# Normalising softmax probabilities on GpSimd: one two-operand multiply of 128x512, or four multiplies by a scalar of 128x128

## The reference, cut to what matters

```python
x = x + xattn(layernorm(x), ctx, ctx, q_norm_w, k_norm_w, w_out)
x = x + ffn(layernorm(x), ...)           # 512 -> 2048 -> 512, 4-bit weights, LoRA terms
# inside xattn: 16 query heads of 32 channels, 4 key/value heads
scores = where(causal, einsum('bgnqd,bgkd->bgnqk', q, k) * scale, -1e30)
attn   = softmax(scores, axis=-1)        # 16 heads x 128 queries x 128 keys a batch
out    = einsum('bgnqk,bgkd->bgnqd', attn, v)
```

## Time and profile before

| what | value |
|---|---|
| three runs | 483.17, 485.31, 486.15 us; median 485.31 us |
| the profiled execution's own time | 484.46 us |
| its span, first to last instruction | 482.7 us, so 1.8 us lie around it |
| busy: DVE, ACT | 352.0 us (73%), 300.3 us (62%) |
| mean granted TensorE clock | 0.979 |
| multiply by the inverse sums (L506), all 64 | 72.7 us of POOL |
| low part of the probabilities (L515), all 64 | 80.9 us of POOL |
| cast of the probabilities (L722), all 64 | 39.7 us of ACT |

### The profile page before, as it was taken

The page is one execution under the profiler, slowest core; times in us unless marked ns, Lnnn a source line. Parts: engine busy times, 40 slices in busy tenths (PEclk is TensorE's granted clock), DMA queues, the critical chain, the costliest instruction groups (busy, mean ns, idle before and its releaser), DMA issues.

```text
span 482.7 us, 8285 instructions
## 1 busy us (share of the span) xinstructions
PE 443.0 (92%) x2416; PEld 218.2 (45%) x2416; DVE 352.0 (73%) x1076; ACT 300.3 (62%) x927; POOL 282.1 (58%) x304
## 2 busy tenths in 40 slices
PE   0285869999999999999999999999999999999997
PEld 0164545444444444444444444444444445444443
DVE  3899998979879786868686877778777856534341
ACT  1698978878858675757575757666675856422120
POOL 5477767685859574848384747576657745451100
PEclk9996879999999999999999999999999999999999
DMA  8679769789777858887867777897697777474422
GB/s 224 215 245 175 189 206 209 114 167 141 160 121 137 168 109 160 135 171 114 171 130 155 134 158 132 169 132 161 122 135 163 118 153 110 91 125 93 88 56 74
DMA packets 207740, 70.36 MB, mean 146 GB/s; under 512 B 196880, under 2 KB 200096, under 8 KB 207056
## 3 DMA queue, kind: packets, MB, share of 16 engines
q1 hardware_dynamic: 206864, 69.35, 72.7%
q10 hardware_dynamic: 752, 0.34, 0.3%
q0 software_dynamic: 80, 0.16, 0.2%
HBM read 17.15 MB, written 4.19 MB: 44 GB/s over the span
## 4 chain that ended last, share of the span: by engine, by line
PE 78%; DVE 1%; DMA 1%; SPq 0%; issue 0%
PE ff L951 33%; PE ff L937 33%; PE tb L919 8%; PE sb L891 2%; PE tb L907 2%; DMA x<-hid 1%; SPq L401 0%; PE tb L877 0%; DVE t_sin L1171 0%; DVE pr L1203 0%; DVE y L1253 0%; DVE stats L1184 0%; DVE x L1181 0%; DVE q L1212 0%; DVE q L1118 0%
## 5 line engine op out<-in xcount | busy, mean ns | idle before, releaser
L951 PE MATMUL ff<-wd_hi,x 128*128 128x512 f16 x512 | 152.3, 379 | 0.7 <-DMA x<-hid 0.7
L937 PE MATMUL ff<-wu_hi,xnT 128*128 128x512 f16 x512 | 152.7, 380 | 0.0
L691 ACT ACTIVATE pr<-pr,nmax 128x128 f32<-128x128 f32 x256 | 99.0, 389 | 13.6 <-DVE nmax L1203 12.9
L515 POOL TENSOR_TENSOR big<-pr,big 128x512 f16<-128x512 f32 x64 | 80.9, 1272 | 32.6 <-ACT big L722 32.6
L937 PE MATMUL ff<-wu_lo,xnT 128*128 128x512 f16 x256 | 97.0, 379 | 0.0
L951 PE MATMUL ff<-wd_lo,x 128*128 128x512 f16 x256 | 97.0, 379 | 0.0
L506 POOL TENSOR_TENSOR pr<-pr,rinv 128x512 f32<-128x512 f32 x64 | 72.7, 1137 | 35.6 <-DVE rinv L1111 35.6
L756 ACT ACTIVATE hid<-z 128x512 f16<-128x512 f32 x64 | 39.9, 624 | 80.1 <-DVE z L1132 80.1
L1203 DVE CUSTOM_DVE_ANT_0 pr<-sb,tabs,score_scale 128x128 f32<-128x128 f32 x256 | 73.8, 344 | 12.3 <-PE sb L891 11.2
L937 PEld LDWEIGHTS ff<-wu_hi,xnT 128*128 128x128 f16 x512 | 48.2, 98 | 58.4 <-issue 5.9
L1132 DVE SCALAR_TENSOR_TENSOR z<-ff,su,b_row 128x512 f32<-128x512 f32 x64 | 47.7, 745 | 36.0 <-PE ff L937 34.7
(11 more groups left out here) (144 smaller groups left out, 652.7 us busy)
## 6 DMA issues: line engine op xcount, KB each, us to landing
xt<-in_x SPq DMA_DIRECT2D x16, 256.0 KB, 3.0
big<-in_L_ffn_w_up_q SPq DMA_DIRECT2D x4, 1024.0 KB, 7.3
big<-in_L_ffn_w_down_q SPq DMA_DIRECT2D x4, 1024.0 KB, 6.2
out<-y SPq DMA_DIRECT2D x16, 256.0 KB, 2.7
wd_lo<-in_L_xattn_w_out SPq DMA_DIRECT2D x1, 1024.0 KB, 7.5
pT<-big SPq DMA_TRANSPOSE x64, 3.5
b_row<-in_L_ffn_b_up SPq DMA_DIRECT2D x1, 1024.0 KB, 9.1
x<-hid SPq DMA_TRANSPOSE x64, 3.2
```

Source lines behind the costliest of these rows:

```text
L515: pool.tensor_tensor(p3[:, m, :, 1, :], pr[:, m], p3[:, m, :, 0, :], ALU.subtract).then_inc(p_low, 1)
L691: last = act.activation(pr[:, m, g, :], pr[:, m, g, :], ACT.Exp, bias=nmax[:, p, j:j + 1], scale=-1.0, accum_out=rsum[:, p, j:j + 1])
L937: last = pe.matmul(bank[:], a[:, m, :], b[:, m, 512 * g:512 * g + 512], start=(m == 0 and i == 0), stop=(m == KC - 1 and i == 2))
L951: last = pe.matmul(ff[down_bank[n]][:], x2T[:, part, k + h % HG, :], b[:, h, :], start=(h == 0 and i == 0), stop=(h == HC - 1 and i == 2))
```

## The change

Each group of probabilities is multiplied on GpSimd in four instructions, one for each head. Each reads one 128 x 128 tensor, and the inverse sum comes as a scalar per partition (a pointer to one column of `rinv`). Before, one instruction read the whole group and a second operand of the same extent, broadcast from four columns of `rinv`. Each piece raises `probs` by one, so ACT waits for four times the count; nothing is moved in any engine's order.

```diff
@@ probabilities(s), on POOL @@
                         pool.wait_ge(inv_sums, 4 * n + m + 1)
-                        pool.tensor_tensor(pr[:, m], pr[:, m],
-                                           rinv[:, p, 4 * m:4 * m + 4].unsqueeze(2).broadcast_to([P, NG, P]),
-                                           ALU.mult).then_inc(probs, 1)
+                        for h in range(NG):
+                            pool.tensor_scalar(pr[:, m, h, :], pr[:, m, h, :], rinv[:, p, 4 * m + h:4 * m + h + 1], None,
+                                               ALU.mult).then_inc(probs, 1)
@@ attention(s), on ACT @@
-                        act.wait_ge(probs, 4 * n + m + 1)
+                        act.wait_ge(probs, 4 * (4 * n + m + 1))
```

## The result

The changed kernel takes 494.83 us (median of four runs, 492.83 to 495.36) against 485.6 us for the kernel before in the same comparison (483.17 to 486.15): ratio 1.0193, 95% interval 1.0162 to 1.0225. It is slower by 9.2 us, where no change was forecast, and lies outside the range given, 482.6 to 488.7 us. The profiled execution took 492.83 us, 8.4 over the one before; its span grew from 482.7 to 490.7 us.

A forecast was written before the change was run, and what follows sets the result against it. The prediction took TensorE, solid from 104 us on, to bound the kernel; POOL's +0.28 us a group cost 0 in batches 0, 1, 2 and the steady state, so 485.3 us was forecast, range 482.6 to 488.7 us.

The forecast's parts named there:

- What bounds the kernel: From 104 us on TensorE alone, without a hole; only a POOL result reaching it too late could lengthen the run there.
- The price of a piece: On POOL: 0.36 us a piece, from a 0.619 us one-tensor row corrected for size and pointer; a group +0.28 us.
- The upper bound of 0.69 us: On POOL: the dearest small instruction, a power of two elements, as price of a piece; a group 2.64 us, +1.60.
- Rival B: Pieces on POOL as dear as a power, a group +1.60 us; 490.4 us, clearly slower; chance 0.09.
- batch 0: Groups 2 and 3, 0.56 us longer, against POOL's idle 1.46 us before the last low part: cost 0.
- batch 2: Tightest place: three groups need 0.84 us of 1.42 us room before the product with the values: cost 0.
- Batch 1: One group ahead of an idle 0.61 us before POOL's last low part: cost 0 below 0.61.
- The steady state: Batches 3 to 15: 1.12 us more a batch, under 2.9 us of room and wiped out by 4.89 us idle: 0.
- exponentials and casts for a queue that has this same room: What stands on ACT behind its cast waiting for POOL; each wait grows 0.28 us, no gain or loss.
- The link that the prediction measured: Steady state: last low parts end at 279.52 us, SP issues their transposes at 282.39; 2.9 us of room.
- A: Pointer scalar on POOL read like a second operand, 0.46 us a piece, a group +0.68; 486.0 us; chance 0.15.
- C: Short pieces collide less with DVE over SBUF, gaining up to 1.7 us; 483.6 us; chance 0.07.

The follow-up runs named there:

- e9: Changed kernel with a second operation (times 1.0) in each of the four pieces: 483.2 us, ratio 0.9984 to the kernel before.
- e3: Changed kernel with each piece a two-operand multiply, the inverse sum broadcast along the row, no pointer: 484.63 us, ratio 1.0003 to the kernel before.
- e5: Kernel before with the four pieces in batches 0 to 2 alone: 489.0 us, ratio 1.0102 to the kernel before.
- e11: Kernel before with the four pieces in batch 0 alone: 485.95 us, ratio 1.0030 to the kernel before.
- e7: Changed kernel with SP's loads issued ahead of the second norm's transpose from batch 3 on: 491.18 us, ratio 1.0147 to the kernel before.
- e8: Kernel before with SP's loads issued ahead of the second norm's transpose from batch 3 on: 482.89 us, ratio 0.9989 to the unmoved kernel before.
- e16: Changed kernel with ACT's cast of the third group issued behind the second norm from batch 3 on: 489.83 us, ratio 1.0123 to the kernel before.
- e10: Changed kernel with one 128x512 instruction a group, add 0 and multiply by 128, both constants: 483.45 us, ratio 0.9988 to the kernel before.
- e2: Changed kernel with one 128x512 pointer-scalar instruction a group in place of four pieces: 483.52 us, ratio 0.9986 to the kernel before.

## Why the prediction was wrong, point by point

**What bounds the kernel** was read right: TensorE solid from 104 us, so that the change could cost there only by making a result late. It cost in the start and in the steady state, the two places that the prediction looked at, but in good part by another path than the one it followed.

**The price of a piece** is the term that was mis-sized first: 0.36 us forecast, 0.605 measured, a group 1.31 us longer and not 0.28. Its terms were good. Size and pointer scaled as taken, for e9 measures 0.371 us on 128 columns with a pointer. What failed is the choice of the nearest row: the step called the row of 0.619 us "the nearest in kind", but that instruction adds and multiplies, while the new one only multiplies. The one-operation form costs 0.23 us more at 128 columns, and the trace of before had no POOL row of it. The upper bound of 0.69 us, from the power, did hold it. The number of operations was not among the differences weighed.

The Trainium skill (GPSIMD Engine Reference, section 4.1) calls one input roughly line rate. The runs agree for two operations, 0.617 us for 512 columns or 1.2 ns each, and not for one, at 2.5 ns an element. Cutting up by itself did not decide: e3's four pieces are 0.43 us a group over one instruction of the same kind, and the time was the same.

**The start.** Rival B's arithmetic, 2 x d - 1.46 at batch 0 and 3 x d - 1.42 at batch 2, gives 1.2 and 2.5 us with the measured d of 1.31; the single-batch runs gave 1.5 and 2.1. Batch 1, 0.61 us of room for one group, adds 0.7, and the trace has a hole of 1.06 us there, where before had none. In sum 4.4 against 4.9 us (by the ratio of e5). The sum comes near partly by luck. At batch 0 the room of 1.46 us ahead of the low part was not what decided: ACT waited 2.02 us at the cast of the third group, the weights' casts stood behind it, and TensorE lost its time at their matmul (e11). The prediction's paragraph on batch 0 has nothing of that queue. At batch 2 the path was the one it named, but the hole is 1.64 us and not 2.5, with a last transpose that lands 1.1 us sooner after its issue. Where the rest of batch 2's 2.1 us is lost isn't shown.

**The steady state** is the step whose path was wrong: "wiped out each time by the 4.89 us, so nothing accumulates". With the true price it claims 5.2 us a batch against 2.9 and 4.89 us of room; the runs show two links that it missed:

- The idle 4.89 us is no reserve. It ends with a load that SP issues behind the second norm's transpose, which needs POOL's own power. Delay POOL and the load comes later too. Moving the loads took back 0.46% of the 1.93% (e7), and removed the idle time there (e7), and three quarters of it in the kernel before (e8).
- Behind ACT's waiting cast the prediction named "exponentials and casts for a queue that has this same room". There also stand the hidden layer and the second norm. Moving the one cast removed every hole of the steady state with the pieces as long as ever (e16), so the whole late half of the loss went through this link.

The link that the prediction measured, low part to SP to the product with the values, is where three of the holes show, 2.3 us. But these went too, with the loads first (e7) and with the cast later (e16), at the same length of piece: what came late there had been delayed by the other two links.

**The rivals.** B, the dear piece, is what happened, with 0.09 of the chance; it was worked out to 490.4 us, with batch 1 left out (1.60 - 0.61 = 0.99 us by its own rule) and the steady state's part named but not priced. A, a pointer read like a second operand, is not the reason for the length: pieces that really have two operands take 0.398 us (e3), less than its 0.46, and cost nothing. Nor is 0.46 us a fixed part, as it says: the 398 and 1041 ns of 128 and 512 columns leave 0.18 us. C, relief for DVE, is not seen: groups that read one tensor in place of two (e9, e10; e9's are longer than before, e10's shorter) came out 0.1 to 0.2% under before, with intervals that touch or include 1.

**The range.** Its low end does not follow from its own words: rival C's 483.6 less the 2.1 us from the median to the lowest run is 481.5, not 482.6. Nothing hangs on it here.

Open: whether the 0.1 to 0.2% are real; how much of the loss passes through DVE's longer busy time (352.0 to 357.6 us; e2, e3, e9 and e10, without a loss, have 346.7 to 351.4), which no run held fixed; and why POOL's one-operation form is the slower one, which the runs show but don't explain.

## What to carry to other kernels

Price a new instruction by the row of the same form, operations counted and not only tensors, and when no such row exists, let the forecast's range go up to the dear bound. Idle time ahead of a wait is room only if what ends the wait does not depend on the engine itself: follow the transfer back through its queue first. When an instruction will make another engine wait longer, list by name everything behind that wait up to the next batch; here one cast moved behind the second norm removed every hole of the steady state. A sum that comes out near the measured time does not show its path: batch 0's did, and TensorE had lost the time at another matmul.

## What the runs showed of the hardware

POOL's `tensor_scalar` in float32 is slower with one operation than with two: on 128x128 with a pointer 605 against 371 ns; on 128x512, 1568 (one operation, pointer) against 617 ns (two, constants). The pointer costs 79 ns a piece (605 against 526). The two-operand multiply with a broadcast second operand takes 398 ns on 128x128, less than the 0.46 us with two full operands, and 1041 ns on 128x512; with two full operands (L538) 128x512 takes 1267 ns at best. So a needless second operation, a multiply by 1.0, is the cheaper way to scale 128x128 by a scalar per partition there (371 against 605 ns).
